# Whole products instead of four column blocks in the second scan, and scatters that wait for a tanh

## The reference, cut to what matters

```python
xp = jnp.einsum('ntd,dh->nth', x, Wx) + b
def step(prev_h, xp_t):
    next_h = jnp.tanh(xp_t + prev_h @ Wh)
    return (next_h, next_h)
_, h = jax.lax.scan(step, h0, jnp.swapaxes(xp, 0, 1))
...
router_logits = jnp.einsum('bnc,ec->bne', x, router_w)       # x is here the h above
expert_weights, expert_idx = jax.lax.top_k(router_probs, TOP_K)
```

## Time and profile before

| what | value |
|---|---|
| median of three runs | 723.65 us (723.62 to 724.5) |
| the profiled execution's own time | 724.12 us |
| its span | 722.0 us |
| mean granted TensorE clock | 0.901 |
| busy share PE / PEld / DVE / ACT / POOL | 83 / 63 / 60 / 54 / 55% |
| second scan, from its first to its last product | about 425.4 to 552.1 us of the span |

### The profile page before, as it was taken

One profiled execution on the slowest core, in us unless ns is written; L12 is line 12 of the kernel. 1 busy time (PEld: TensorE's weight loads), 2 busy tenths in 40 slices (PEclk: granted clock), 3 DMA queues, 4 the chain that ended last, 5 costly groups with the idle time before them and its releaser, 6 DMA issues. The chain is left out here.

```text
span 722.0 us, 27247 instructions
## 1 busy us (share of the span) xinstructions
PE 600.2 (83%) x10479; PEld 454.5 (63%) x10479; DVE 434.7 (60%) x2041; ACT 391.0 (54%) x1112; POOL 400.6 (55%) x459
## 2 busy tenths in 40 slices
PE   3888888888879999999998777767766988999993
PEld 1565555555667777676766653434334878899993
DVE  1666666666557688678866325455554744454687
ACT  4666666666414555555554423222224767788893
POOL 4445554445338888788877421444443677655552
PEclk9999999999989999999999968555555999999997
DMA  7356655555686876576665033332111123222653
GB/s 254 118 206 227 227 187 210 206 205 195 236 249 189 223 201 194 156 210 193 188 174 184 4 143 102 108 113 73 36 43 43 52 74 90 71 69 69 206 183 112
DMA packets 111946, 108.73 MB, mean 151 GB/s; under 512 B 7136, under 2 KB 85472, under 8 KB 111440
## 3 DMA queue, kind: packets, MB, share of 16 engines
q1 hardware_dynamic: 107120, 97.66, 42.7%
q0 software_dynamic: 4320, 8.89, 3.7%
q10 hardware_dynamic: 384, 0.52, 0.2%
HBM read 59.43 MB, written 45.52 MB: 145 GB/s over the span
## 5 line engine op out<-in xcount | busy, mean ns | idle before, releaser
L515 POOL TENSOR_TENSOR sc<-sc,mx 128x1024 f32<-128x1024 f32 x64 | 121.1, 1897 | 50.4 <-DVE mx L673 50.4
L406 POOL TENSOR_SCALAR QD<-q_all,mask 128x128 f32<-128x128 f32 x126 | 88.5, 714 | 98.4 <-DVE pre L361 95.1
L673 DVE CUSTOM_DVE_ANT_0 sc<-banks,s2t 128x128 f32<-128x128 f32 x512 | 112.1, 286 | 46.1 <-PE banks L566 44.7
L1213 POOL DMA_INDIRECT expert_outputs<-yr,xr x71 | 73.2, 1030 | 63.0 <-DVE yr L1487 38.9
L1198 POOL DMA_INDIRECT expert_inputs<-rows,slotu x64 | 62.7, 980 | 75.6 <-PE banks L420 71.3
L731 ACT ACTIVATE PT<-banks 128x512 f32<-128x512 f32 x128 | 69.6, 596 | 62.1 <-PE banks L579 62.1
L1146 ACT ACTIVATE hid<-banks,w1b 128x128 f32<-128x128 f32 x284 | 80.5, 366 | 24.3 <-PE banks L1089 19.3
L352 DVE COPY s2stage<-banks 128x512 f32<-128x512 f32 (+1 forms) x90 | 76.6, 852 | 16.6 <-PE banks L253 16.6
L1128 ACT ACTIVATE h<-banks,bias 128x32 f32<-128x32 f32 x128 | 36.8, 287 | 91.0 <-PE banks L420 88.2
L253 PE MATMUL banks<-RK,QD 32*128 32x128 f32 x1024 | 78.5, 454 | 3.9 <-DVE s2stage L352 0.9
L1089 PE MATMUL banks<-xt,w1b 128*128 128x128 f32 x568 | 79.3, 284 | 2.8 <-DVE xt L1437 2.8
(11 more groups left out here) (145 smaller groups left out, 1071.9 us busy)
## 6 DMA issues: line engine op xcount, KB each, us to landing
s_scratch<-s2stage SPq DMA_DIRECT2D x32, 1024.0 KB, 4.8
s2t<-s_scratch SPq DMA_DIRECT2D x64, 512.0 KB, 4.8
xr<-expert_inputs SPq DMA_DIRECT2D x71, 64.5 KB
xz<-in_xz SPq DMA_DIRECT2D x8, 512.0 KB, 5.8
yb<-expert_outputs SPq DMA_DIRECT2D x16, 256.0 KB
w2all<-in_w2b SPq DMA_DIRECT2D x8, 320.0 KB
w1a<-in_w1b SPq DMA_DIRECT2D x8, 258.0 KB
k_all<-in_xT SPq DMA_DIRECT2D x1, 2048.0 KB, 10.6
```

Of the source, the lines that this page charges most:

```text
L406: op = pool.tensor_scalar(QD[G % 3][:, :, h, :], q_all[:, :, quad(G)].rearrange("p b t -> p t b"), mask[:, h:h + 1], None, ALU.mult)
L515: pool.tensor_tensor(sc[U % RING][:], sc[U % RING][:], mx[U % RING][:].unsqueeze(2).broadcast_to([P, HH, T]), ALU.subtract)\
L673: op = dve.tensor_tensor_reduce(out=sc[r][:, h, :], in0=ps[2 * (U % 2) + h // 4][:, h % 4 * T:(h % 4 + 1) * T], in1=s2t[r][:, h, :], scale ...
L1213: pool.indirect_dma_start(yg_dram, bass.IndirectOffsetOnAxis(xr[k][:, D:].bitcast(U32), 0), yr[k][:], None).then_inc(s_ys[k], 16)
```

## The change

A new helper `whole_product` issues one matmul with all 128 columns of the weights. Every product of the second scan except the state's uses it: inputs, output projection, rows of states, logits, positions. The state's product stays in four column blocks. And the scatters wait for `s_h2` in place of `s_r`, with the same number.

```diff
+        def whole_product(pe, bank, lo, hi, w, moving, first=True, last=True):
+            return pe.matmul(ps[bank][:, lo:hi], w[:, 0:P], moving, start=first, stop=last, skip_group_check=True)
+
         def inputs_of_scan2(pe, m, w, columns, lo, n, first):
-            return column_products(pe, m % 2, lo * B, (lo + n) * B, w,
+            return whole_product(pe, m % 2, lo * B, (lo + n) * B, w,
                                    columns[:, m * TC + lo:m * TC + lo + n, :], first and lo == 0, False)
...
-                                mm = column_products(pe, 6 - m % 2, k * P, (k + 1) * P, outputs, wo[:])
+                                mm = whole_product(pe, 6 - m % 2, k * P, (k + 1) * P, outputs, wo[:])
...
-                            mm = column_products(pe, at_rt, k * P, (k + 1) * P, states(o, k), ident[:])
+                            mm = whole_product(pe, at_rt, k * P, (k + 1) * P, states(o, k), ident[:])
...
-                    mm = column_products(pe, 2 if c < NCH - 1 else 7, k * E, (k + 1) * E, states(c % 2, k), rwT[:])
+                    mm = whole_product(pe, 2 if c < NCH - 1 else 7, k * E, (k + 1) * E, states(c % 2, k), rwT[:])
...
-                    column_products(pe, bank, lo, lo + JT * E, upper, chosen)
-                    column_products(pe, bank, lo + JT * E, lo + 2 * JT * E, ones, chosen).then_inc(s_pos, 1)
+                    whole_product(pe, bank, lo, lo + JT * E, upper, chosen)
+                    whole_product(pe, bank, lo + JT * E, lo + 2 * JT * E, ones, chosen).then_inc(s_pos, 1)
...
                     for k in range(2 * JT):
                         if scatter_step(c, k) < T:
-                            pool.wait_ge(s_r, scatter_step(c, k) + 1)
+                            pool.wait_ge(s_h2, scatter_step(c, k) + 1)
                             scatter(c, k)
```

## The result

| | before | after |
|---|---|---|
| median of 4 runs | 723.76 us (723.62 to 724.5) | 736.12 us (734.48 to 738.33) |
| ratio | 1 | 1.0176, 95% interval 1.0141 to 1.021 |
| profiled execution, time / span | 724.12 / 722.0 | 737.71 / 735.1 |
| second scan, first to last state's product | 125.86 us | 136.65 us |
| tanhs of the scan that came late, and by how much in all | 60, 31 us | 5, 1.3 us |

The changed kernel is slower by 12.4 us. The forecast was 748 with a range of 722 to 760. The sign and the range held, but the sum came out 12 us lower, and a rival that I had given 0.12 (the holds go) is what the trace shows.

What follows compares the result with a forecast made beforehand. The second scan's circle of product, tanh, product was taken as the bound. Step times of 133.7 plus 17 us of scatter delays, less 126.7 now, gave +24: 746.0 of span, 748 us with 2.1 around it; range 722 to 760.

Steps and rivals of the forecast that it cites:

- the holds go: Second scan: an earlier scatter start lets the product's signal pass, no tanh is delayed; +7, 731 us; chance 0.12.
- What bounds the kernel: Second scan: the circle product, tanh, product; of ACT's 88.2 us of waits 56 are this circle, 32 the scatters.
- Switches: Second scan: changing between column and whole matmuls delays the weights load to 0.07 us before the end; steps 0.75 become 1.00.
- Logits and positions: Second scan: as whole products they add 0.20 us to a step with logits and 0.55 for positions: 1.20 and 1.55.
- The holds: Second scan: scatters still delay the tanhs due after them, 0.68 of them long; 17 us, bounds 0 and 34.
- floors: Second scan: step times without scatter delays, summing to 133.7 us where the stage now takes 126.7.
- The holds get longer: Second scan: all 51 scatters delay a tanh until 1.55 us after their start; 34 us, +41, 765 us; chance 0.08.
- The clock rises: Second scan: fuller TensorE queue brings the full clock, the stage takes 110 us, 17 less, 707 us; chance 0.14.
- The switches cost nothing: Second scan: PE pulls loads ahead, only the scatter's shift is left; +17, 741 us, or 692 without holds; chance 0.06.
- TensorE's waiting: Theory from the follow-ups, second scan: a signal is held only when TensorE itself stands waiting for the tanh; no chance given.

Runs made afterwards that it cites:

- the split kernel: The kernel before, with each product of 128 moving columns cut into four column products of 32: 753.9 us, ratio 1.1018.

## Why the prediction was right, and where it was not

**What bounds the kernel: right.** The forecast took 56 us of ACT's waits for the chain and 32 for holds. Step by step the late time of that trace is 31 us. On chip C, where the holds are all but absent, the row for the same kernel says 56.0; that it hits the 56 to the decimal is luck, since most of its waits are 0.39 us at the full clock and not 0.45.

**Switches: right.** Forecast and measured: plain step 1.00 and 0.993; load 0.07 before the end of what runs ahead, seen in the changed kernel, and gone when nothing changes the tiling (the kernel with all products whole). The drain is shown. It is the cause of the slower kernel: whole products cost the stage 41 us in all, and the holds give only 30 of them back.

**Logits and positions: slightly too low.** 1.20 against 1.22, but 1.42 where the logits stand between the state's product and another whole product; positions 1.55 against 1.69; a chunk 17.35 against 17.69. With its late tanhs taken off, the stage is 136.4 where the same ends gave 133.7 in the forecast (427.4 to 565.1 is 137.7, less 1.3). That is 2.7 us, 2.0 of them in chunks 1 to 6.

**The holds: this term failed.** It was 17 us and measured 1.3, and nearly the whole miss is here: the stage took 137.7 us for the 150.7 of the forecast, 15.7 less by the holds and 2.7 more by its floors. The step that failed is the last sentence of its working: "I take 17, since the start relative to the product differs by only 0.05 us from the one the rows have." The place of the scatter is not what decides on chip A. With whole products the tanh passes with the scatter 0.03 before its product and with the scatter 0.35 before it (the wait on `s_r` restored); with column blocks it is held in both places, 0.10 before the product and (the next one) 0.52 before it. I had carried a duration from a kernel whose other instructions were different, and changed only its phase. The lower bound, "no hold at all, 0", was nearly the case. The direction did not hang on this term, since the floors alone gave +7; the size did: the forecast rise of 24 us is twice the measured one.

**The rivals.** *The holds go*, 731 us and 0.12, is the nearest in time: +7 forecast, +13.1 in the profiled span, which is 7, 2.7 by which the floors were too low, 1.3 for the holds that are left, 1.9 for the later start of the stage and 0.2 behind it. Its reason, the earlier start of the scatter, is not needed: with the wait on `s_r` restored the holds are gone as well. *The holds get longer* (34 us) is refuted by the same 1.3. *The clock rises* did not happen in either trace of the changed kernel; what the forecast did not have is the reverse, that the clock of the kernel before can be high and that the change takes it away (chip C). *The switches cost nothing* is refuted.

**What stays open.** Why whole products free the signals on chip A. TensorE's waiting stays a rival. No kernel on chip A tests it: with all products whole a filling product is still loading when the signal falls due, and only 7 of its signals fell due where those of column kernels are held, six of them at about 0.95. What speaks against it is one signal of the last chunk of the changed kernel, held by 0.37 while a whole product was being loaded. The same signal speaks against the tiling theory, that a column product's signal is held unless a whole one stands behind it; otherwise that theory fits most rows, though in the kernel before 5 of 51 were not late with column products behind them. The number of instructions per us differs between the groups too (43 against 20). The kernels meant to part these ran on chips B and C, and the long holds of the first trace were seen on neither. Why the kernel before is without them on chip C, and at the full clock there, is open as well.

## What to carry to other kernels

On TensorE, price a change of tiling by the first weights load behind it (here it waits until 0.07 us before the end of what is ahead), and count it twice per step; small products pay it too (0.19 us for one of the router's here, 0.28 for one with 128 columns), and leaving them in column blocks took the change from 1.018 to 1.005. A net of 11 us can be 41 lost and 30 gained. A delay that one engine inflicts on another is a property of the whole instruction stream and of the chip: before it is put into a sum, take one part of the change alone and look at the same kernel on a second chip. This program, bound by a chain of short steps, was nearly 6% apart between chips (723.6 and 683 to 684 us), so a ratio measured on one chip (1.018) need not be that of another (1.068).

Of the versions tried, only the kernel before with the scatters' wait on `s_h2` was faster than the kernel before, by 0.4% on chip A (0.9957, 0.9928 to 0.9986); on the other two chips it was not run.

## What the runs showed of the hardware that I had not expected

- **The same program on three chips.** The kernel before: 723.61, 684.09 and 683.24 us. The parts are 31 against 0.3 us of late signals in the second scan, and 22 against 101 state's products at the full clock (first trace against chip C). The changed kernel differs much less (736.12 and 730.3).
- **TensorE can run out of instructions.** Where the program asks for 107 loads and matmuls per us, stops of about 1 to 3 us come every 256 instructions, 52.7 us in 37 waits, and 69 per us are what gets through; in the kernel before on chip C (32 per 0.68 us, 47 per us) TensorE waits so only four times from 447 to 504 us, 2.0 us in all and 0.7 at most.
- **A scatter's hold ends at one of two times, and the long one was not seen on every chip.** In the first trace 13 of the 46 late signals were released 0.58 to 0.67 us after the scatter's start and most of the others at 1.3 to 1.45; on A, with only the wait changed, 39 of 42 at 1.33 to 1.54. On B, in the split kernel, nearly all were released at 0.65 to 0.84, and on C the few late ones behind a scatter at 0.64 to 0.74.
